# Order of VectorE's last instructions in a graph attention and mixture-of-experts kernel

## The chip, the cores and the metric

One core of one Trainium2 chip runs the whole program. The metric is the device time of one execution in microseconds (us). The engines are TensorE (PE, with its weight loads as PEld), VectorE (DVE), ScalarE (ACT), GpSimd (POOL) and SyncE (SP, which issues most DMAs). Each has its own queue of instructions, and they meet by semaphores.

## The reference

A layer of graph attention on 384 nodes of width 1024 comes first; the change does not touch it. Then comes a mixture of 8 experts, of which each token takes 2:

```python
def _expert(x, g, b, W1, b1, W2, b2, Wo, bo):
    x = _layernorm(x, g, b)
    x1 = x @ W1 + b1
    x2 = jnp.clip(x @ W2 + b2, -20.0, 20.0)
    hidden = jnp.clip(x1 * (x2 * jax.nn.sigmoid(x2)), -10000.0, 10000.0)
    return jnp.clip(hidden @ Wo + bo, -10000.0, 10000.0)
...
scores, idx = jax.lax.top_k(logits, K)
gate = jax.nn.softmax(scores, axis=-1)
...
return (acc + gcol[:, None] * _expert(xf, g, b, w1, bb1, w2, bb2, wo, bbo), None)
...
x = x + _L0_ffn_ref(_layernorm(x, axis=-1)[None], ...)[0]
```

Everything is float32. D is 1024, the hidden width H is 512.

## The kernel before, in words

**Products in two parts.** A float32 operand is split into a high part (`hi`, of a shorter type, copied by ScalarE) and the rest (`lo`, subtracted by VectorE). A product is three matmuls: high by high, high by low, low by high (`three`, line 1206, its matmul on line 1209). The weights come in chunks of 128x2048 (1 MB): SyncE loads a chunk into a raw buffer, ScalarE copies it to `hi` (`split_hi`, line 577, its operation on 581), VectorE subtracts (`split_lo`, line 776, its operation on 778). There are 76 chunks; expert 7's are 68 to 71 (up), and 74 and 75 (down); 72 and 73 are expert 6's down chunks.

**The experts.** Each takes the at most 128 tokens that chose it. For expert `e` TensorE (loop from line 1456) makes the two up projections into banks 1 and 0, then the down projection of expert `e - 1` into banks 3 and 4 (`down`, line 1433: two bias products of line 1439, then per chunk twelve matmuls of line 1209), then turns the hidden activations of expert `e` into bank 2 (line 1451). ScalarE copies bank 2 to the high activations (line 708), VectorE subtracts the low ones (`hidden_lo`, line 1079, operation on 1081). VectorE clips banks 3 and 4 into `y` (`store_y`, line 1084, operation on 1089). `down` waits for the low activations of its expert and for the clip of the expert before (`y_ready`), since both use banks 3 and 4. Then it waits for each of its chunks.

**Adding up.** The outputs of experts 0 to 5 are written to HBM (`ybuf`) by SyncE. Each token gathers its rows back: six gathers of 128 rows (`gather_rows`, line 513, its DMA on 515, issued by GpSimd; three tiles of tokens, two choices each), numbered 0 to 5. VectorE multiplies four of them by the gate and adds them to the residual `xres` (`add_rows`, line 1139, operation on 1143). The gathers 4 and 5 are scaled by ScalarE (line 740) and added to `xres` by GpSimd (line 555).

The outputs of experts 6 and 7 don't go through HBM. They are brought to the tokens by products with one-hot matrices: VectorE builds these (line 1113), TensorE turns them (line 1476) and also makes two columns of gates with twelve one-column products (line 1479); ScalarE copies the turned matrices (line 730), VectorE copies the gate columns (line 1153, `slot_gates`). Expert 6's rows `y` are split with their gate into high rows (ScalarE, line 734) and low rows (VectorE, `y_rest`, line 1146, operation on 1147). Expert 7's rows are clipped in two halves (VectorE, line 1162), then split by halves (ScalarE, line 744; VectorE, `y_rest`). TensorE sums them in six banks (`add_last`, line 1483, matmuls on 1490). VectorE adds the six banks to `xres` (line 1171), and SyncE stores a piece behind each addition (line 423).

**What sets the order.** Each engine's instructions are written out by hand in the order in which it runs them. On VectorE the end is: the clip of the hidden activations of expert 7 (line 1134), splits 74 and 75 (line 1137), low activations of expert 7, clip of expert 6's rows, gate columns, the additions 0, 1 and 2, low rows of expert 6, addition 3, the two clips of expert 7 (which wait for all chunks to be used), the two low halves, and the last six additions. On ScalarE it is: the high activations of expert 7 (708), the turned matrices (730), the high rows of expert 6 (734), the scaling of gathers 4 and 5 (740), the two high halves (744).

Of the kernel before, what the change touches and what calls it, by code (L numbers as in the profile page):

```python
# [41 lines left out]
D = 1024  # L42
# [6 lines left out]
NE = 8  # L49
# [28 lines left out]
CHUNKS = GNN_CHUNKS + len(EXPERT_ORDER)  # L78
# [28 lines left out]
def gnn_ffn(nc, x, src, dst, ety, srcb, dstb, ew, wg, bcols, bo, lng, lnb, lnbc_in, rw, egc, ebc, wf, b1, b2, be, out):  # L107
    ctx = ExitStack()
    with ctx:
        def sem(name):  # L110
            return ctx.enter_context(nc.semaphore(name))
# [147 lines left out]
        slot_gates, y_half, y_hi_done, y_lo_done = sem("slot_gates"), sem("y_half"), sem("y_hi_done"), sem("y_lo_done")  # L259
# [10 lines left out]
        def f0(e):  # L270


            return GNN_CHUNKS + 6 * e - 2

        def up_chunks(e):
            return f0(e) + (2 if e == 0 else 0)
# [51 lines left out]
        def f32(ap):  # L328
            return ap.bitcast(F32)

        def wait_lo(engine, c):

            engine.wait_ge(lo_done, c + 1)
# [434 lines left out]
        def _(dve):  # L768
            chain = [0]

            def link(ins):
                chain[0] += 1
                ins.then_inc(dve_chain, 1)
                dve.wait_ge(dve_chain, chain[0])

            def split_lo(c):
                dve.wait_ge(hi_done, c + 1)
                dve.tensor_tensor(lo[SLOT[c]][:, :], raws[RAW[c]], f32(hi[SLOT[c]][:, :]), ALU.subtract).then_inc(lo_done, 1)  # L778
# [269 lines left out]
            def row_columns():  # L1048

                for j, oh in enumerate((oh1, oh2)):  # L1050
                    link(dve.tensor_tensor(tmp[early], oh[early], pos[early], ALU.mult))
                    link(dve.tensor_reduce(r3[:, 5, :], tmp[early], AX, ALU.add))
                    link(dve.tensor_tensor(tmp[early], oh[early], first_row[early], ALU.mult))
                    link(dve.tensor_reduce(r3[:, 6, :], tmp[early], AX, ALU.add))
                    link(dve.scalar_tensor_tensor(out=r3[:, 3 + j, :], in0=r3[:, 5, :], scalar=float(CAP - 1),
                                                  in1=r3[:, 6, :], op0=ALU.min, op1=ALU.add))
                dve.tensor_copy(rows_u[:, :, :], r3[:, 3:5, :]).then_inc(rows_u_ready, 1)

            def gate_columns():

                dve.wait_ge(gates_ready, 1)
                link(dve.tensor_tensor(over_gate, oh1, wide(r3[:, 8, :]), ALU.mult))
                link(dve.tensor_tensor(tmp, oh2, wide(r3[:, 9, :]), ALU.mult))
                link(dve.tensor_tensor(tmp, tmp, over_gate, ALU.add))
                link(dve.scalar_tensor_tensor(out=over_gate, in0=pos, scalar=float(CAP), in1=tmp, op0=ALU.is_ge, op1=ALU.mult))
                link(dve.scalar_tensor_tensor(out=gates, in0=pos, scalar=float(CAP), in1=tmp, op0=ALU.is_lt, op1=ALU.mult))
                for j, oh in enumerate((oh1, oh2)):
                    link(dve.tensor_tensor(tmp[early], oh[early], gates[early], ALU.mult))
                    link(dve.tensor_reduce(r3[:, 8 + j, :], tmp[early], AX, ALU.add))
                dve.tensor_copy(most[:, :], r3[:, 2, 0:1]).then_inc(most_ready, 1)  # L1070

            def tokens_lo(e, par):
                for a in range(2):
                    half = slice(4 * a, 4 * a + 4)
                    dve.wait_ge(xg_hi_done, 2 * e + a + 1)
                    dve.tensor_tensor(xg_lo[:, par, half, :].rearrange("p k n -> p (k n)"), xg[:, par, a * CW:(a + 1) * CW],
                                      f32(xg_hi[:, par, half, :]).rearrange("p k n -> p (k n)"), ALU.subtract).then_inc(xg_lo_done, 1)

            def hidden_lo(e, par):
                dve.wait_ge(ht_hi_done, e + 1)  # L1080
                dve.tensor_tensor(ht_lo[:, par, :, :].rearrange("p k n -> p (k n)"), B[2],
                                  f32(ht_hi[:, par, :, :]).rearrange("p k n -> p (k n)"), ALU.subtract).then_inc(ht_lo_done, 1)

            def store_y(e, par):

                dve.wait_ge(chunk_used, f0(e + 1) + 6 if e < NE - 1 else CHUNKS)
                if e >= 2:
                    dve.wait_ge(y_stored[par], 16 * (e // 2))
                dve.tensor_scalar(y[:, par, :].rearrange("p (a n) -> p a n", a=2), ps[:, 3:5, :], 10000.0, -10000.0,
                                  ALU.min, ALU.max).then_inc(y_ready, 1)  # L1090
# [9 lines left out]
            for e in range(NE):  # L1100
                nxt = [k if FIRST <= k < CHUNKS else None for k in range(f0(e) + 3, f0(e) + 9)]
                if e:
                    hidden_lo(e - 1, (e - 1) % 2)
                if e >= 2:
                    store_y(e - 2, e % 2)
                if nxt[0]:
                    split_lo(nxt[0])
                if e == NE - 1:

                    wait_lo(dve, UP_LAST)  # L1110
                    for j in range(2):
                        for t in range(NT):
                            ins = dve.tensor_scalar(last_rows[:, j, t, :], slots16[:, :], posm[:, t, LAST[j]:LAST[j] + 1], None, ALU.is_equal)
                    ins.then_inc(last_oh, 1)
                if nxt[1]:
                    split_lo(nxt[1])
                if e == 0:
                    row_columns()
                dve.wait_ge(chunk_used, up_chunks(e) + 2)
                if e:  # L1120
                    dve.wait_ge(h_ready, e)
                dve.tensor_scalar(x2c[:, :], B[1], 20.0, -20.0, ALU.min, ALU.max).then_inc(x2_clipped, 1)
                if e == 0:
                    gate_columns()
                if nxt[2]:
                    split_lo(nxt[2])
                if e + 1 < NE:
                    tokens_lo(e + 1, (e + 1) % 2)
                dve.wait_ge(silu_done, e + 1)
                dve.wait_ge(chunk_used, up_chunks(e) + 4)  # L1130
                if e:
                    dve.wait_ge(h_turned, e)
                link(dve.tensor_tensor(hh[:, :], B[0], sg[:, :], ALU.mult))
                dve.tensor_scalar(hh[:, :], hh[:, :], 10000.0, -10000.0, ALU.min, ALU.max).then_inc(h_ready, 1)
                for k in nxt[3:6]:
                    if k:
                        split_lo(k)

            def add_rows(n):

                t, j = GATHERS[n]
                dve.wait_ge(y_rows_in[j][t], 16)
                link(dve.scalar_tensor_tensor(out=xres[:, t, :], in0=yg[:, YG_SLOT[n], :], scalar=r3[:, 8 + j, t:t + 1],
                                              in1=xres[:, t, :], op0=ALU.mult, op1=ALU.add))

            def y_rest(e, cut):
                dve.scalar_tensor_tensor(out=y_lo[e][:, cut], in0=y[:, e, cut], scalar=slot_gate[:, e:e + 1], in1=f32(y_hi[e][:, cut]),
                                         op0=ALU.mult, op1=ALU.subtract).then_inc(y_lo_done, 1)

            hidden_lo(NE - 1, (NE - 1) % 2)  # L1150
            store_y(NE - 2, (NE - 2) % 2)
            dve.wait_ge(last_oh_turned, 1)
            dve.tensor_copy(slot_gate, B[7][:, 0:2]).then_inc(slot_gates, 1)
            for n in range(3):
                add_rows(n)
            dve.wait_ge(y_hi_done, 1)
            y_rest(0, slice(0, D))
            add_rows(3)
            dve.wait_ge(chunk_used, CHUNKS)
            halves = [slice(0, CW), slice(CW, D)]  # L1160
            for half in range(2):
# [1 line left out]
            for half in range(2):  # L1163
                dve.wait_ge(y_hi_done, 2 + half)
                y_rest(1, halves[half])
            for half in range(2):
                for t in range(NT):
                    dve.wait_ge(last_summed, NT * half + t + 1)
                    if t == NT - 1:
                        dve.wait_ge(tile_added, 1)  # L1170
                    dve.tensor_tensor(xres[:, t, halves[half]], xres[:, t, halves[half]], B[SUM_BANKS[t][half]],
                                      ALU.add).then_inc(out_ready, 1)
# [407 lines left out]
```

## Time and profile before

| what | us |
|---|---|
| three runs | 516.27, 519.77, 518.66 |
| their median | 518.66 |
| the profiled execution's own time | 518.99 |
| its span, from the first to the last instruction | 517.2 |

| engine | busy, share of the span |
|---|---|
| TensorE, matmuls | 93% |
| VectorE | 74% |
| ScalarE | 53% |
| GpSimd | 33% |

The span is what the views of the trace show; the profiled execution's own time is 1.8 us more. A line of a timeline has the start, the duration, the engine, the line of the code, the operation, what is written and read, the shapes and the count; in brackets stands the idle time of the engine before it and what ended that. The duration of merged lines is that from the first start to the last end. Consecutive instructions of VectorE overlap by some hundredths of a microsecond, so a row of 0.68 costs the next one some 0.6 to 0.65. The granted clock of TensorE is 1.00 at 2.4 GHz and 0.50 at 1.2 GHz.

### The profile page before, as it was taken

What the parts mean: (1) busy time and instruction counts of PE and PEld (TensorE: products, weight loads), DVE (VectorE), ACT (ScalarE), POOL (GpSimd) and SP (SyncE); (2) the same over time, 40 slices, a digit from 0 to 9 for tenths busy, and PEclk for the clock granted to TensorE, in tenths of its full rate; (3) what the DMA queues carried; (4) which work ended last, traced back from release to release, by engine and by line L of the source; (5) the groups of instructions that cost most, each with busy time, mean ns of one, the idle gap of its engine ahead of it and who ended that gap; (6) DMA issues with size and microseconds to landing.
All of it is one profiled execution on the core that took longest, in us unless ns stands there. A gap on an engine that the chain in (4) does not pass through costs nothing.

```text
span 517.2 us, 6811 instructions
## 1 busy us (share of the span) xinstructions
PE 482.4 (93%) x2599; PEld 414.2 (80%) x2599; DVE 382.4 (74%) x616; ACT 274.1 (53%) x382; POOL 171.6 (33%) x152
## 2 busy tenths in 40 slices
PE   8999999999999999978899999588999999999984
PEld 8999999999999987755656788467887787877772
DVE  4858989955353342478877987787898898898985
ACT  4725142423433243378785035249769669669531
POOL 5000543764645200456765532420201000000561
PEclk9999999999999999999999998579999999999988
DMA  8489655442424532200055733685788989987553
GB/s 294 161 307 376 167 196 220 164 163 86 148 93 164 169 122 81 81 1 2 1 168 217 284 123 122 207 308 209 303 324 362 398 330 403 352 302 323 182 182 124
DMA packets 21073, 106.33 MB, mean 206 GB/s; under 512 B 4864, under 2 KB 5248, under 8 KB 11312
## 3 DMA queue, kind: packets, MB, share of 16 engines
q1 hardware_dynamic: 15472, 91.53, 47.2%
q0 software_dynamic: 3696, 7.96, 4.8%
q10 hardware_dynamic: 1872, 6.39, 3.7%
q8 instruction: 21, 0.34, 0.3%
q14 instruction: 12, 0.10, 0.1%
HBM read 98.97 MB, written 6.91 MB: 205 GB/s over the span
## 4 chain that ended last, share of the span: by engine, by line
PE 58%; DVE 22%; ACT 10%; DMA 4%; issue 4%; POOL 0%; SPq 0%; DVEq 0%; ACTq 0%; POOLq 0%
PE ps L1209 45%; DVE lo L778 11%; ACT hi L581 4%; ACT xg L695 3%; PE ps L1289 3%; PE ps L1272 3%; PE ps L1300 2%; DMA raw<-in_wg 2%; PE ps L1317 2%; DVE eqt L861 1%; PE ps L1369 1%; DVE pr L878 1%; ACT pr L617 1%; DMA raw<-in_wf 1%; DMA xg<-z_rows,slot_tok 1%
## 5 line engine op out<-in xcount | busy, mean ns | idle before, releaser
L778 DVE TENSOR_TENSOR lo<-raw,hi 128x2048 fp32r<-128x2048 f32 x70 | 161.4, 2328 | 40.4 <-ACT hi L581 40.2
L581 ACT ACTIVATE hi<-raw 128x2048 fp32r<-128x2048 f32 x70 | 131.8, 1913 | 59.0 <-PE ps L1209 46.2
L466 POOL DMA_INDIRECT mask_rows<-colf,bits x48 | 63.1, 1315 | 90.9 <-DVE bits L869 43.6
L497 POOL TENSOR_SCALAR pr<-pr,small 128x384 f32<-128x384 f32 x32 | 40.4, 1275 | 57.8 <-DVE small L884 57.8
L1209 PE MATMUL ps<-xt_hi,lo 128*128 128x384 f32 x176 | 59.1, 336 | 0.0
L1209 PE MATMUL ps<-xt_hi,hi 128*128 128x384 f32 x176 | 59.1, 336 | 0.0
L1209 PE MATMUL ps<-xt_lo,hi 128*128 128x384 f32 x176 | 59.1, 336 | 0.0
L1209 PE MATMUL ps<-hi,xg_hi 128*128 128x512 f32 x128 | 52.0, 406 | 5.7 <-DVE lo L778 3.9
L1209 PE MATMUL ps<-lo,xg_hi 128*128 128x512 f32 x128 | 51.1, 400 | 0.0
L1209 PE MATMUL ps<-hi,xg_lo 128*128 128x512 f32 x128 | 51.1, 399 | 0.0
L1209 PE MATMUL ps<-t_hi,hi 128*128 128x384 f32 x128 | 43.1, 337 | 0.8 <-DVE t_lo L820 0.8
L1209 PE MATMUL ps<-t_hi,lo 128*128 128x384 f32 x128 | 43.0, 336 | 0.0
L1209 PE MATMUL ps<-t_lo,hi 128*128 128x384 f32 x128 | 43.0, 336 | 0.0
L1209 PE MATMUL ps<-hi,t_hi 128*128 128x512 f32 x96 | 39.8, 414 | 0.0
L1209 PE MATMUL ps<-hi,t_lo 128*128 128x512 f32 x96 | 37.9, 395 | 0.0
L1209 PE MATMUL ps<-lo,t_hi 128*128 128x512 f32 x96 | 37.9, 394 | 0.0
L617 ACT ACTIVATE pr<-pr,small 128x384 f32<-128x384 f32 x48 | 29.0, 607 | 14.4 <-DVE small L878 14.4
L1209 PEld LDWEIGHTS ps<-hi,xg_hi 128*128 128x128 f32 x128 | 24.6, 192 | 12.8 <-DVE lo L778 5.4
L525 POOL CAST selx<-sels 128x128 fp32r<-128x128 f32 x8 | 4.4, 551 | 87.3 <-PE ps L1209 86.5
L1209 PEld LDWEIGHTS ps<-xt_hi,lo 128*128 128x128 f32 x176 | 33.1, 188 | 0.0
L1209 PEld LDWEIGHTS ps<-xt_hi,hi 128*128 128x128 f32 x176 | 33.1, 188 | 0.0
L1209 PEld LDWEIGHTS ps<-xt_lo,hi 128*128 128x128 f32 x176 | 33.1, 188 | 0.0
(218 smaller groups left out, 966.8 us busy)
## 6 DMA issues: line engine op xcount, KB each, us to landing
raw<-in_wf SPq DMA_DIRECT2D x42, 1024.0 KB, 7.8
raw<-in_wg SPq DMA_DIRECT2D x28, 1024.0 KB, 4.9
xfb<-in_wf SPq DMA_DIRECT2D x6, 1024.0 KB, 7.2
src_i<-in_srcb ACTq DMA_DIRECT2D x4, 768.0 KB, 3.9
dst_i<-in_dstb ACTq DMA_DIRECT2D x4, 768.0 KB, 7.8
y_rows<-y SPq DMA_DIRECT2D x6, 512.0 KB, 3.0
xin<-in_x SPq DMA_DIRECT2D x3, 512.0 KB, 4.3
xres<-in_x SPq DMA_DIRECT2D x3, 512.0 KB, 4.2
```

The costliest lines, as they stand in the source:

```text
L466: pool.indirect_dma_start(out=mbuf[:, :], out_offset=bass.IndirectOffsetOnAxis(ap=bits[:, 1, g:g + 1], axis=0), in_=colf[:, 5, g:g + 1], i ...
L497: pool.tensor_scalar(pr[:, p % 3, a, i, :], pr[:, p % 3, a, i, :], rinv[:, p % 3, i, a:a + 1], None, ALU.mult).then_inc(normalised, 1)
L581: act.activation(hi[SLOT[c]][:, :], raws[RAW[c]], ACT.Copy).then_inc(hi_done, 1)
L617: act.activation(pr[:, p % 3, a, i, :], pr[:, p % 3, a, i, :], ACT.Exp, scale=-1.0, bias=negmax[:, p % 3, i, a:a + 1], accum_out=rsum[:, p ...
L695: ins = act.activation(xg[:, par, k * P:(k + 1) * P], B[5 + a][:, (k % 4) * P:(k % 4 + 1) * P], ACT.Identity, scale=egb[:, 0, e, k:k + 1], ...
L778: dve.tensor_tensor(lo[SLOT[c]][:, :], raws[RAW[c]], f32(hi[SLOT[c]][:, :]), ALU.subtract).then_inc(lo_done, 1)
L861: ins = dve.scalar_tensor_tensor(out=eqt[:, j % 2, 0:width], in0=keyb[:, j * P:j * P + width], scalar=colf[:, 2, g:g + 1], in1=later[:, 0: ...
L1209: ins = pe.matmul(o, a[s], b[m], start=first and n == 0, stop=last and n == 2)
L1272: ins = pe.matmul(SCORES[n % 2][a][:, 0:N], (q_hi, q_lo)[s][rows, p, tok], (k_hi, k_lo)[m][rows, p, :], start=step == 0, stop=step == 2)
L1289: ins = pe.transpose(TURNED[m % 3][:, i * P:(i + 1) * P], pr[:, p % 3, a, i, j * P:(j + 1) * P], ident[:, :])
L1300: ins = pe.matmul(SUMMED[HD * a:HD * (a + 1), 0:N], val[:, j, cut], at[:, m % 8, :], start=j == 0, stop=j == NT - 1)
L1317: ins = pe.matmul(banks(0)[b][:, 0:N], weight(0, k, slice(b * P, (b + 1) * P))[s], (xt_hi, xt_lo)[m][:, k, :], start=n == 0 and k == 0, st ...
```

## The change

Only VectorE's program changes. In the loop of the experts, the last weight split (chunk 75) is left out. Behind the loop the clip of expert 6's rows now comes first, then the low activations of expert 7, the gate columns, split 75, the low rows of expert 6, the additions 0, 1 and 2. The fourth addition (`add_rows(3)`) moves from behind the low rows of expert 6 to behind the two low halves of expert 7.

```diff
                 for k in nxt[3:6]:
-                    if k:
+                    if k and k < CHUNKS - 1:
                         split_lo(k)
...
+            store_y(NE - 2, (NE - 2) % 2)
             hidden_lo(NE - 1, (NE - 1) % 2)
-            store_y(NE - 2, (NE - 2) % 2)
             dve.wait_ge(last_oh_turned, 1)
             dve.tensor_copy(slot_gate, B[7][:, 0:2]).then_inc(slot_gates, 1)
+            split_lo(CHUNKS - 1)
+            dve.wait_ge(y_hi_done, 1)
+            y_rest(0, slice(0, D))
             for n in range(3):
                 add_rows(n)
-            dve.wait_ge(y_hi_done, 1)
-            y_rest(0, slice(0, D))
-            add_rows(3)
             dve.wait_ge(chunk_used, CHUNKS)
             halves = [slice(0, CW), slice(CW, D)]
             for half in range(2):
...
             for half in range(2):
                 dve.wait_ge(y_hi_done, 2 + half)
                 y_rest(1, halves[half])
+            add_rows(3)
             for half in range(2):
                 for t in range(NT):
                     dve.wait_ge(last_summed, NT * half + t + 1)
```

## Rows read from the trace of the kernel before

**Rows 1.** The page, busy time of each engine

```profile
PE 482.4 (93%) x2599; PEld 414.2 (80%) x2599; DVE 382.4 (74%) x616; ACT 274.1 (53%) x382; POOL 171.6 (33%) x152
```

**Rows 2.** Chain of waits that ended last (start, us, what), from 440 us

```profile
466.87 2.80 PE ps L1209 x12
...
494.55 1.22 DVE y L1089
...
496.61 7.16 PE ps L1209 x24
...
505.35 2.13 DVE lo L1147
```

**Rows 3.** Timeline of VectorE, from 470 us

```profile
489.55 4.48 DVE L778 TENSOR_TENSOR lo<-raw,hi 128x2048 fp32r<-128x2048 f32 x2
493.95 0.68 DVE L1081 TENSOR_TENSOR ht_lo<-ps,ht_hi 128x512 fp32r<-128x512 f32 x1
494.55 1.21 DVE L1089 TENSOR_SCALAR y<-ps 128x1024 f32<-128x1024 f32 x1
...
495.75 3.91 DVE L1143 SCALAR_TENSOR_TENSOR xres<-yg,r,xres 128x1024 f32<-128x1024 f32 x3
...
500.90 1.28 DVE L1143 SCALAR_TENSOR_TENSOR xres<-yg,r,xres 128x1024 f32<-128x1024 f32 x1
503.87 1.29 DVE L1162 TENSOR_SCALAR y<-ps 128x512 f32<-128x512 f32 x2 [1.68 <-PE ps L1209]
...
508.30 3.67 DVE L1171 TENSOR_TENSOR xres<-xres,ps 128x512 f32<-128x512 f32 x6 [0.17 <-PE ps L1490]
```

**Rows 4.** Timeline of TensorE, from 470 us

```profile
491.28 0.40 PE L1209 MATMUL ps<-hi,ht_lo 128*128 128x512 f32 x1
...
492.61 1.40 PE L1479 MATMUL ps<-r,xfb 128*128 128x1 f32 x12
495.91 0.70 PE L1439 MATMUL ps<-brow,selx 128*128 128x512 f32 x2 [1.91 <-DVE y L1089]
```

**Rows 5.** One stretch: us, busy (count) by engine, granted clock (PEclk), DMA, GB/s

```profile
498.00:499.00 1.00, 1.00 (x4) 0.80 (x3) 0.96 (x2) 0.00 (x0) 0.00 (x0) 0.50 1.06 360
```

**Rows 6.** Timeline of ScalarE, from 470 us

```profile
492.15 0.60 ACT L708 ACTIVATE ht_hi<-ps 128x512 fp32r<-128x512 f32 x1 [1.50 <-PE ps L1451]
494.04 0.87 ACT L730 ACTIVATE hi<-ps 128x384 fp32r<-128x384 f32 x2 [1.29 <-PE ps L1479]
...
500.47 1.16 ACT L740 ACTIVATE yg<-yg,r 128x1024 f32<-128x1024 f32 x1 [3.44 <-DMA yg<-y_rows,rows_u]
501.94 1.15 ACT L740 ACTIVATE yg<-yg,r 128x1024 f32<-128x1024 f32 x1 [0.31 <-DMA yg<-y_rows,rows_u]
504.59 1.34 ACT L744 ACTIVATE hi<-y,r 128x512 fp32r<-128x512 f32 x2 [1.50 <-DVE y L1162]
```

**Rows 7.** Timeline of GpSimd: the last three gathers' issue, and its two additions

```profile
492.95 1.90 POOL L515 DMA_INDIRECT yg<-y_rows,rows_u  x1 [0.30 <-issue]
495.15 0.94 POOL L515 DMA_INDIRECT yg<-y_rows,rows_u  x1 [0.30 <-issue]
496.40 1.44 POOL L515 DMA_INDIRECT yg<-y_rows,rows_u  x1 [0.30 <-issue]
501.71 2.74 POOL L555 TENSOR_TENSOR xres<-xres,yg 128x1024 f32<-128x1024 f32 x1 [3.87 <-ACT yg L740]
504.54 2.38 POOL L555 TENSOR_TENSOR xres<-xres,yg 128x1024 f32<-128x1024 f32 x1
```

**Rows 8.** View of line 515, the six gathers: from issue to landing

```profile
DMA to landing us min/median/max: 5.2/6.0/6.3
```

**Rows 9.** Timelines of GpSimd and VectorE from 283 us, outside the change

```profile
283.35 2.39 POOL L490 TENSOR_TENSOR xres<-xres,x2sg 128x1024 f32<-128x1024 f32 x1 [2.68 <-DVE lo L778]
...
285.69 4.47 POOL L490 TENSOR_TENSOR xres<-xres,x2sg 128x1024 f32<-128x1024 f32 x1
...
283.50 4.40 DVE L778 TENSOR_TENSOR lo<-raw,hi 128x2048 fp32r<-128x2048 f32 x1 [0.23 <-ACT hi L581]
```

## The prediction

> **What bounds the kernel now.** I read the page first: TensorE is busy for 93% of the span [rows 1], so elsewhere in the program time on VectorE matters only where TensorE waits for it. The change touches only the last 28 us, so I read the chain of waits there. The reader is to see that it changes engines: it runs over VectorE's clip of expert 6's rows (494.55), TensorE's last 24 weight products, then VectorE's first low half (505.35) [rows 2]. The timeline of each engine then shows why.
>
> VectorE is without a gap from 489.55 to 502.18, has one gap of 1.68 us before 503.87 (it waits for TensorE), and ends its last addition at 508.30 + 3.67 = 511.97 [rows 3]. TensorE stands idle for 1.91 us before 495.91, since its last down projection needs expert 6's rows clipped out of banks 3 and 4, and the clip stands behind two splits on VectorE [rows 3, 4]. After that gap the granted clock is 0.50 in 498 to 499, 1.2 of 2.4 GHz [rows 5]. So 24 products with their two bias products take 503.8 - 495.9 = 7.9 us, where twelve at the full clock took 2.80 us earlier [rows 2]: 24 would be 5.6.
>
> ScalarE and GpSimd are the third part. Behind TensorE's end VectorE clips two halves, but ScalarE's high halves can only follow when it has scaled the two gathered tiles whose rows landed at 500.47 and 501.94 [rows 6]. GpSimd adds these tiles to the residual, from 501.71 and from 504.54 [rows 7].
>
> **The change, step by step.** Nothing is added or removed: the same instructions stand in another order on one engine. No DMA is issued by the moved code; SP's queue waits for nothing that moves except the last six additions; GpSimd's queue holds no moved instruction, but I come to it.
>
> 1. *Clip and low half ahead of split 75.* VectorE ends split 74 at 489.55 + 2.28 = 491.8. TensorE's last product of expert 6 ends at 491.28 + 0.40 = 491.7 [rows 4], so the clip starts at 491.8 at once and is done at 493.0 (1.21 [rows 3]). The high half of the activations is there at 492.15 + 0.60 = 492.75 [rows 6]; the low half takes 0.65 and ends at 493.65 [rows 3]. Now a wait stands ahead of split 75: the copy of the two gate columns needs TensorE's twelve column products, which end at 492.61 + 1.40 = 494.0 [rows 4]. So VectorE idles 0.4 us, and behind that wait stands split 75, 494.1 to 496.4.
>
> 2. *TensorE.* Both things it waited for are there at 493.65, so it starts when its own queue is through, at 494.05 in place of 495.91: 1.85 us sooner. It needs chunk 75 after its two bias products (0.7) and twelve others (2.8), at 497.55; the split ends at 496.4. That is 1.15 us of cover; a split later than that would cost what it is late. I take the full clock, since the gap that came before the half clock is gone: end at 494.05 + 0.7 + 5.6 = 500.35, 3.4 us sooner. At the half clock for as long as before it is 1.6 more, 501.95. Both ends are covered, as step 4 shows.
>
> 3. *VectorE up to the clips.* ScalarE's first high rows come at 494.04 + 0.87 + 1.16 = 496.1 (two copies, then a tile of 1.16 as at 500.47 [rows 6]). So the low rows of expert 6 (1.28, as an addition of their size [rows 3]) follow the split without a wait, 496.35 to 497.6, and three additions of 1.28 bring VectorE to 501.5 (3.91 for three [rows 3]). This is later than TensorE's 500.35: the gap of 1.68 is gone and VectorE is what is late next. The two clips run 501.5 to 502.8, 2.35 us sooner than before.
>
> 4. *What is late after that: ScalarE, through the gathers.* The gathers' own issue on GpSimd takes 0.94 when VectorE reads PSUM (495.15, under the clip). It is held while VectorE runs a split: the one from 492.95 ended at 494.85, 0.8 after the split that ended at 494.03; the one from 496.40 ended 0.8 after an addition had ended at 497.03 [rows 3, 7]. In the new order the fourth gather lies under the clip and the low half and ends at 493.9; the fifth starts at 494.2, just behind the start of split 75 at 494.1, and is held until 496.4 + 0.8 = 497.2; the sixth lies under the low rows, 497.5 to 498.4. From issue to landing the six took 5.2 to 6.3 us [rows 8]. For the fifth, held as long as any, I take 6.3: 500.5, as before. The sixth lands near 502. ScalarE scales the fifth by 501.7 and the sixth by 503.2, and only then makes the high halves, to 504.6. So TensorE's 3.4 us and VectorE's 2.35 us arrive at ScalarE as little more than 1.4 (504.59 before [rows 6]).
>
> 5. *The two additions of GpSimd and the low halves.* In the trace before, the first low half took 2.13 us at 128x512, where 1.28 buys twice the size on an addition: it stood from 505.35 until GpSimd's second addition had ended at 504.54 + 2.38 = 506.92, then took 0.6 [rows 2, 7]. The same pair of kinds meets earlier in the trace: at 283.50 a split waited 2.1 us for GpSimd's addition from 283.35, and then GpSimd's next, from 285.69, waited 2.1 us for that split [rows 9]. So one holds off the other, and whoever waits comes in between two instructions of the other engine. Put in order: GpSimd's first addition 501.8 to 504.2; first low half (asked for at 503.95) 504.2 to 504.85; GpSimd's second 504.85 to 507.25; second low half to 507.9. If GpSimd's second comes ahead of both halves, the sum is the same, since the four simply queue. Before, it was 508.13: a gain of 0.2 is left. The price per half lies between 0 and 2.38; I take the queue, because both rows above show it for these kinds.
>
> 6. *The fourth addition moved behind the halves.* Before it lay ahead of VectorE's gap of 1.68 and cost nothing. Its new place is on the path: 507.9 + 1.28 = 509.2. TensorE's last sums would be ready by then (first half from 504.9 on), so nothing covers it. The last six additions follow, 3.67: 512.85, against 511.97.
>
> Sum: -0.2 (halves), -0.15 (the wait of the last additions), +1.28 (fourth addition) = **+0.9 us**. The rest of the span after the last addition (517.2 - 511.97, the last stores) stays. The profiled execution's own time was 518.99, so it would be 519.9; that one lies 0.33 above the median of the three runs, 518.66, and by the median I say **519.6 us**.
>
> At step 4 the trace and a rule differ. [Rows 7] show the gathers' issue held by splits and additions that VectorE makes of two SBUF operands. The Trainium skill ("SBUF — State Buffer", section "Who interferes with whom") says of VectorE's `tensor_tensor` that it "takes only the pair's read interface, and descriptor generation needs the write interface: inferred"; by it the fifth gather would not be held. What that gives is worked out from rows as the second rival below. The measurement decides here, and it says held; the chance of the rival comes from how close 494.1 and 494.2 are.
>
> **The rivals.** *The low halves don't queue with GpSimd* (faster). Then the halves end at 505.2, the fourth addition at 506.5, the last at 510.15: -1.8 us, 516.8. For it: the clips, read from PSUM, took 0.65 each (1.29 for both) under GpSimd's first addition, undisturbed [rows 3, 7], and the halves need only come in other moments. Against it: both rows of step 5.
>
> *The fifth gather gets in ahead of split 75.* Then it takes 0.94 and lands 5.2 us after 494.2, at 499.4; ScalarE is done with it at 500.55, but VectorE's third addition runs to 501.5 and holds GpSimd's off until then. First addition 501.5 to 503.9, first half 504.55, second addition 506.9, second half 507.55, fourth addition 508.85, last 512.5: +0.5, 519.2. For it: 0.1 us decides. Against it: GpSimd would have to be early.
>
> *The last gathers land later* (slower). Everything in step 5 hangs on the start of GpSimd's first addition, one us for one us, from 501.8 on. The fifth gather now leaves GpSimd 1.1 us later than before (497.2 against 496.1), and before it landed 4.4 us after leaving. By that it lands at 501.6, the first addition starts at 502.85 and the last ends at 513.9: +1.9, 520.6. For it: 4.1 and 4.4 are the times from leaving to landing of the last two [rows 6, 7]. Against it: those two stood behind other gathers' rows, and the fifth no longer does.
>
> *The change doesn't do what it says:* TensorE's gap stays, because the column products and not the clip end last, or split 75 is late by more than 1.15 us. Then TensorE ends as before, the clips come at 503.8, the halves as before at 508.1, and the fourth addition still costs 1.28: +1.1, 519.8. The products' end at 494.0 speaks against it.
>
> **How the numbers follow.** Forecast (+0.9) 0.50; halves not queued (-1.8) 0.18; fifth gather first (+0.5) 0.14; gathers late (+1.9) 0.15; gap stays (+1.1) 0.03. The cases span 516.8 to 520.6. The three runs lie between 2.4 below and 1.1 above their median, and I add a part of this at either end: 516.0 to 521.5; the forecast's own range is 518.6 to 520.6. About 1%, 5.2 us, is what a measurement of this kernel can tell from no change. No case reaches it: even all 3.4 us of TensorE would not. Outside lie surprises alone, 0.02 faster and 0.03 slower.
>
> **What would show it.** Right: TensorE's bias products of line 1439 start near 494.05 with no idle time before them; the granted clock stays at 1.00 to 501; no idle time on VectorE before line 1162, which starts near 501.5; a low half of line 1147 of some 2.4 to 3 us beside GpSimd's line 555; the fourth addition ending near 509.2. Wrong: both low halves at 0.65 and the last addition before 511; the fifth gather issued in 0.94; an idle gap inside TensorE's 24 products; a time outside 516 to 521.5.

## The result, and the profile after

The changed kernel took 520.75 us by the median of 22 runs, against 518.86 of 22 runs of the kernel before: a ratio of 1.0031 (1.0021 to 1.0042), 1.1 to 2.2 us more. That is no change by the bound of 1%, and slower by what so many runs can tell. Two later comparisons of the same pair, with 12 runs of the changed kernel each, gave 1.0017 (0.9998 to 1.0036) and 1.0012 (0.9996 to 1.0028). The forecast was 519.6, +0.9 us; the profiled execution after has a span of 518.3 against 517.2.

The changed kernel has one line more ahead of VectorE's last additions and of TensorE's code, so TensorE's 1209, 1439 and 1490 are now 1210, 1440 and 1491, and VectorE's 1171 is 1172. This is the timeline of VectorE after (start, duration, then as before), which answers to [rows 3]:

```profile
489.60 2.28 DVE L778 TENSOR_TENSOR lo<-raw,hi 128x2048 fp32r<-128x2048 f32 x1
491.80 1.22 DVE L1089 TENSOR_SCALAR y<-ps 128x1024 f32<-128x1024 f32 x1
492.93 0.68 DVE L1081 TENSOR_TENSOR ht_lo<-ps,ht_hi 128x512 fp32r<-128x512 f32 x1
494.05 0.16 DVE L1153 COPY r<-ps 128x2 f32<-128x2 f32 x1 [0.44 <-PE ps L1480]
494.12 2.28 DVE L778 TENSOR_TENSOR lo<-raw,hi 128x2048 fp32r<-128x2048 f32 x1
496.32 1.28 DVE L1147 SCALAR_TENSOR_TENSOR lo<-y,r,hi 128x1024 fp32r<-128x1024 f32 x1
497.52 3.92 DVE L1143 SCALAR_TENSOR_TENSOR xres<-yg,r,xres 128x1024 f32<-128x1024 f32 x3
501.48 1.29 DVE L1162 TENSOR_SCALAR y<-ps 128x512 f32<-128x512 f32 x2
504.48 3.51 DVE L1147 SCALAR_TENSOR_TENSOR lo<-y,r,hi 128x512 fp32r<-128x512 f32 x2 [1.71 <-ACT hi L744]
507.91 1.27 DVE L1143 SCALAR_TENSOR_TENSOR xres<-yg,r,xres 128x1024 f32<-128x1024 f32 x1
509.22 3.68 DVE L1172 TENSOR_TENSOR xres<-xres,ps 128x512 f32<-128x512 f32 x6
```

The wait of 1.68 us for TensorE ahead of the clips is gone, and a wait of 1.71 us for ScalarE has come behind them. The clips start 2.4 us sooner; the two low halves, which took 2.78 us under GpSimd's second addition, now take 3.51 and end at 507.99 in place of 508.13. The fourth addition follows them, so the last addition ends at 512.90, not 511.97.

TensorE after, which answers to [rows 4]: no idle time ahead of the bias products, and a new gap ahead of expert 7's sums.

```profile
492.61 1.40 PE L1480 MATMUL ps<-r,xfb 128*128 128x1 f32 x12
493.87 0.71 PE L1440 MATMUL ps<-brow,selx 128*128 128x512 f32 x2
...
499.77 0.39 PE L1210 MATMUL ps<-hi,ht_lo 128*128 128x512 f32 x1
...
507.38 0.79 PE L1491 MATMUL ps<-hi 128*128 128x512 f32 x1 [4.50 <-DVE lo L1147]
```

The down projection ends at 500.16, 3.6 us sooner. That lead ends in a gap of 4.50 us. Two stretches after, with the granted clock third from the right (as [rows 5]):

```profile
497.00:498.00 1.00, 1.00 (x6) 0.82 (x5) 1.00 (x2) 0.00 (x0) 0.70 (x2) 1.00 0.39 98
508.00:509.00 1.00, 1.00 (x4) 0.81 (x3) 1.00 (x1) 0.00 (x0) 0.00 (x0) 0.50 0.00 0
```

In this profile the half clock has not gone but moved: from the 24 products to the sums behind the new gap. Two more profiles of the changed kernel (below) differ here: the sums of the second half run at 0.50 again in one, and in the other the granted clock stays at 1.00, where TensorE waited 2.35 and then 1.13 us. The last two gathers, GpSimd's additions and ScalarE's scaling, which answer to [rows 6, 7]:

```profile
494.24 2.98 POOL L515 DMA_INDIRECT yg<-y_rows,rows_u  x1 [0.30 <-issue]
497.52 0.94 POOL L515 DMA_INDIRECT yg<-y_rows,rows_u  x1 [0.30 <-issue]
502.00 2.36 POOL L555 TENSOR_TENSOR xres<-xres,yg 128x1024 f32<-128x1024 f32 x1 [3.54 <-ACT yg L740]
504.44 2.33 POOL L555 TENSOR_TENSOR xres<-xres,yg 128x1024 f32<-128x1024 f32 x1
```
```profile
500.75 1.16 ACT L740 ACTIVATE yg<-yg,r 128x1024 f32<-128x1024 f32 x1 [4.79 <-DMA yg<-y_rows,rows_u]
502.68 1.15 ACT L740 ACTIVATE yg<-yg,r 128x1024 f32<-128x1024 f32 x1 [0.77 <-DMA yg<-y_rows,rows_u]
```

The fifth gather's issue is held under split 75 (2.98 us, ending 0.82 after the split ended at 496.40). GpSimd's second addition, 504.44 to 506.77, came 0.04 us ahead of the first low half, which stood until it was through.

### The profile page after: what moved, and what is told of

It is laid out like the page before. It is cut to its first block, busy times and chain, and to the rows that moved or that the text cites. A ratio compares the mean times of both kernels' runs of the same rounds, so it can differ in the third digit from the quotient of the medians.

```text
span 518.3 us, 6811 instructions
## 1 busy us (share of the span) xinstructions
PE 481.6 (93%) x2599; PEld 413.6 (80%) x2599; DVE 383.1 (74%) x616; ACT 273.9 (53%) x382; POOL 169.3 (33%) x152
## 4 chain that ended last, share of the span: by engine, by line
PE 55%; DVE 21%; ACT 10%; DMA 6%; issue 4%; POOL 3%; ACTq 0%; SPq 0%; DVEq 0%; POOLq 0%
PE ps L1210 42%; DVE lo L778 10%; ACT hi L581 4%; ACT xg L695 3%; PE ps L1290 3%; PE ps L1273 3%; PE ps L1301 2%; POOL yg L515 2%; DMA raw<-in_wg 2%; PE ps L1318 2%; DVE eqt L861 1%; PE ps L1370 1%; DVE pr L878 1%; DMA yg<-y_rows,rows_u 1%; ACT pr L617 1%
## 5 line engine op out<-in xcount | busy, mean ns | idle before, releaser
L466 POOL DMA_INDIRECT mask_rows<-colf,bits x48 | 61.9, 1290 | 92.5 <-DVE bits L869 44.3
```

The source lines that it names most:

```text
L466: pool.indirect_dma_start(out=mbuf[:, :], out_offset=bass.IndirectOffsetOnAxis(ap=bits[:, 1, g:g + 1], axis=0), in_=colf[:, 5, g:g + 1], i ...
```

## The experiments

Executions reach the tail at times up to 2 us apart, so the profiles are compared from a mark that all share: the start of split 74 (489.55 before). To the end of the last addition it is 22.42 us before and 23.30 after; such figures of each run, worked out from its timelines, stand in the table at the end of this section.

**One part alone: the fourth addition moved, the rest as before.**

```diff
             y_rest(0, slice(0, D))
-            add_rows(3)
             dve.wait_ge(chunk_used, CHUNKS)
...
                 y_rest(1, halves[half])
+            add_rows(3)
```

> The kernel before, with its fourth addition alone moved behind the two low halves. Theory (one queue): the low halves of VectorE and the two additions of GpSimd pass one after the other, so the halves end near 507.9 with or without the addition ahead of them, and its 1.28 us come on top: last addition ends near 512.75, 0.8 us later than before (ratio 1.0015). Rival (the early split is what costs): no difference, within 0.3 us of before, since TensorE, ScalarE and the splits stand as they did. Rival (clock): over 1.3 us later, if TensorE's last sums run at the half clock and end after VectorE.

Ratio 1.0013 (0.9995 to 1.0030); last addition 22.85 us from the mark, 0.43 later than before. The halves end 0.63 sooner from the mark (17.95 against 18.58), and the addition itself costs its 1.27. The sign is as the queue says, the size half; the time alone can't tell it from nothing. The 0.63 has two sources, which this run doesn't part. GpSimd's first addition is no longer held by the fourth of VectorE (2.42 us, not 2.74). And TensorE, after the same wait for the clip as before, keeps the full clock this time (third from the right again), so the clips come 1.64 sooner from the mark and the first low half gets in between GpSimd's two additions:

```profile
497.28 0.70 PE L1439 MATMUL ps<-brow,selx 128*128 128x512 f32 x2 [1.95 <-DVE y L1089]
498.00:499.00 1.00, 1.00 (x6) 0.78 (x6) 0.96 (x2) 0.39 (x1) 1.00 (x1) 1.00 0.93 369
```
```profile
503.60 1.29 DVE L1161 TENSOR_SCALAR y<-ps 128x512 f32<-128x512 f32 x2 [1.25 <-PE ps L1209]
505.09 3.78 DVE L1147 SCALAR_TENSOR_TENSOR lo<-y,r,hi 128x512 fp32r<-128x512 f32 x2 [0.20 <-ACT hi L744]
```

So the half clock of the one profile of before does not follow each such gap, and some 1.6 of the 3.6 us that TensorE gains there came here without the early clip.

**The other part alone: the changed kernel with the fourth addition ahead of the clips.**

```diff
                 add_rows(n)
+            add_rows(3)
             dve.wait_ge(chunk_used, CHUNKS)
...
                 y_rest(1, halves[half])
-            add_rows(3)
```

> The changed kernel with its fourth addition put back ahead of the two clips; the early clip, low activations and late split stay. Theory (one queue): the addition now lies at 501.5 to 502.8 and holds GpSimd's first addition until then; the halves end near 508.8 and the last addition near 512.4: 0.45 us sooner than the changed kernel, 0.45 later than before (ratio 1.0009). Rival (the fourth addition was all the loss): 1.3 us sooner than the changed kernel, level with before or 0.2 better.

Ratio 1.0012 (0.9995 to 1.0030). The last addition ends 22.35 us from the mark: 0.95 sooner than in the changed kernel, level with before. Timeline of its VectorE:

```profile
503.84 1.29 DVE L1163 TENSOR_SCALAR y<-ps 128x512 f32<-128x512 f32 x2
505.50 3.92 DVE L1147 SCALAR_TENSOR_TENSOR lo<-y,r,hi 128x512 fp32r<-128x512 f32 x2 [0.38 <-ACT hi L744]
509.35 3.66 DVE L1172 TENSOR_TENSOR xres<-xres,ps 128x512 f32<-128x512 f32 x6
```

Here the rival was nearer than my theory (0.45): by the profile the moved addition is all of the loss, and the early clip and late split, which gave TensorE 3.6 us, are worth nothing at the end (22.35 against 22.42), with the halves again at 3.92 us in GpSimd's queue. The times alone can't show it: 1.0012 lies inside the intervals of the two later comparisons of the changed kernel.

**GpSimd's additions cut short.**

```diff
-ins = pool.tensor_tensor(xres[:, t, :], xres[:, t, :], yg[:, YG_SLOT[n], :], ALU.add)
+ins = pool.tensor_tensor(xres[:, t, 0:8], xres[:, t, 0:8], yg[:, YG_SLOT[n], 0:8], ALU.add)
```

> The changed kernel with GpSimd's two additions cut to 8 of 1024 columns: most of the sum for one choice of the third tile of tokens is left out. Theory (one queue): nothing holds the low halves, each takes some 0.65; ScalarE gives the first high half at 504.5, so the halves end at 505.8, the fourth addition at 507.1 and the last addition at 510.8: 2.1 us sooner than the changed kernel, 1.2 sooner than before (ratio 0.998). Rival (ScalarE and the landing of the gathers set the end): within 0.3 us of the changed kernel. Rival (clock): some 1 us sooner, since TensorE's last twelve sums at the half clock then end at 510.3 to 510.8 and not VectorE's work.

Ratio 0.9987 (0.9962 to 1.0012). Its VectorE:

```profile
505.88 1.41 DVE L1147 SCALAR_TENSOR_TENSOR lo<-y,r,hi 128x512 fp32r<-128x512 f32 x2 [1.76 <-ACT hi L744]
```

Both halves together now take 1.41 us, not 3.51, and the last addition ends 21.24 from the mark, 2.06 sooner than in the changed kernel: what was expected to 0.1. ScalarE still ends the wait ahead of them, so its part of step 4 stands beside that queue.

**The fourth addition in VectorE's gap.**

```diff
+            add_rows(3)
             for half in range(2):
                 dve.wait_ge(y_hi_done, 2 + half)
                 y_rest(1, halves[half])
-            add_rows(3)
```

> The changed kernel with its fourth addition between the two clips and the low halves, where its VectorE stands idle for 1.7 us. Theory (one queue): the gap is no gap for an addition of two SBUF operands, since GpSimd's first addition runs through it; the fourth addition waits for that, the low halves and GpSimd's second addition queue behind, and the last addition ends within 0.4 us of the changed kernel. Rival (the gap is free): 1.2 us sooner than the changed kernel, 0.3 sooner than before.

Ratio 1.0043 (1.0023 to 1.0063); last addition 24.98 us from the mark, 1.7 later than in the changed kernel. Neither expectation. VectorE:

```profile
502.04 2.88 DVE L1143 SCALAR_TENSOR_TENSOR xres<-yg,r,xres 128x1024 f32<-128x1024 f32 x1
504.95 3.37 DVE L1147 SCALAR_TENSOR_TENSOR lo<-y,r,hi 128x512 fp32r<-128x512 f32 x2
508.97 0.69 DVE L1172 TENSOR_TENSOR xres<-xres,ps 128x512 f32<-128x512 f32 x1 [0.65 <-PE ps L1491]
509.82 0.69 DVE L1172 TENSOR_TENSOR xres<-xres,ps 128x512 f32<-128x512 f32 x1 [0.17 <-PE ps L1491]
...
513.24 0.69 DVE L1172 TENSOR_TENSOR xres<-xres,ps 128x512 f32<-128x512 f32 x1 [0.16 <-PE ps L1491]
```
```profile
508.00:509.00 1.00, 1.00 (x3) 0.81 (x3) 0.35 (x2) 0.00 (x0) 0.00 (x0) 0.50 0.00 0
```

The queue is there: the addition takes 2.88 us in place of 1.28, and the gap was no gap. But TensorE then stands idle for 5.47 us, its sums run at 0.50, and each last addition waits for TensorE and comes 0.86 us after the one before, not 0.6. My theory had left the clock out; here it decides. In the first profile of the changed kernel the sums at the half clock just keep up, because the fourth addition lies ahead of the last six.

**The fifth gather let in ahead of split 75.**

```diff
             dve.wait_ge(last_oh_turned, 1)
+            for _ in range(3):
+                link(dve.tensor_copy(slot_gate, B[7][:, 0:2]))
             dve.tensor_copy(slot_gate, B[7][:, 0:2]).then_inc(slot_gates, 1)
```

> The changed kernel with the copy of the two gate columns made four times over, each waiting for the one ahead, so that split 75 starts some 0.5 us later, behind the start of the fifth gather's issue. Theory (the splits hold the gathers' issue): the fifth gather is issued in 0.94 us and not 2.98, and its rows land 5.2 us after the start of its issue, some 1 us sooner than in the changed kernel; its gain is held back by VectorE's third addition, and the last addition ends within 0.5 us of the changed kernel. Rival (the issue of a gather takes long for another reason, as its own place in the order): 2.5 us or more again.

There is one profile of this version and no comparison of times; last addition 22.92 us from the mark, 0.38 sooner than in the changed kernel, with the added copies in it. Its last two gathers:

```profile
495.05 0.93 POOL L515 DMA_INDIRECT yg<-y_rows,rows_u  x1 [0.30 <-issue]
496.29 2.36 POOL L515 DMA_INDIRECT yg<-y_rows,rows_u  x1 [0.30 <-issue]
```

The fifth takes 0.93, not 2.98, and now the sixth is held under the split (495.56 to 497.84) and leaves 0.81 after it. So a split does hold a gather's issue. The Trainium skill's inference in "SBUF — State Buffer" ("Who interferes with whom"), that a `tensor_tensor` leaves descriptor generation alone, is not borne out by these rows for a gather. Among what the rows of a gather read stands `rows_u`, its row numbers in SBUF; whether that read or the making of descriptors is held they don't show. The rows of the fifth landed only some 0.45 us sooner, 6.1 us after the start of the issue and not 5.2.

**The changed kernel again, plain, twice.**

> The changed kernel once more, beside the others of this call. By its profile, from the start of split 74 to the end of the last addition, it loses 0.9 us to the kernel before (ratio 1.0017); by the first measurement 1.6 (1.0031). Theory (one queue): in a profile the first low half waits for GpSimd's second addition or stands between the two, and the last addition ends some 23.3 us after the start of split 74. Rival (clock): the profile shows TensorE's last twelve sums ending later than VectorE's fourth addition allows, and the last addition with a wait ahead of it.

> The changed kernel a third time, as the measure for the next one. Theory (queue and clock): 0.9 us over before in executions in which TensorE's last sums keep up (ratio 1.0017), up to 2 in those in which they run at the half clock behind a late first half; 1.002 to 1.003 on the whole. A look at its last additions shows which it is: back to back every 0.6 us, or one per 0.86 with a wait on TensorE.

The ratios are given above; last addition 23.69 and 23.28 us from the mark. In both the first low half stands between GpSimd's two additions and the last additions follow each other every 0.6 us. So in three profiles the tail is 0.9 to 1.3 us longer than in the one of before, and in none does TensorE's clock hold up an addition.

**The changed kernel with 16 idle products in TensorE's gap, twice.**

```diff
             add_last(0, (0, 1), True)
+            pe.wait_ge(y_half, 1)
+            keep_busy(16, B[3])
```

> The changed kernel with 16 idle products (0.24 us each) on TensorE between the sums of expert 6 and those of expert 7, so that it doesn't stand idle for 4.5 us. Theory (one queue): VectorE's fourth addition and GpSimd's port set the end; the granted clock stays at 1.00, the last sums are done sooner, and the time stays within 0.3 us of the changed kernel in the same call. Rival (clock): the half clock is the rest of the measured loss; 0.6 us or more sooner than the changed kernel.

> The changed kernel with the 16 idle products again, beside the plain one. Theory (queue and clock): the granted clock stays at 1.00 and every last addition follows the one before; 0.5 to 1.5 us sooner than the plain one in this call. Rival (queue alone): within 0.3 us of it, and the first comparison was chance.

Ratios 0.9987 (0.9971 to 1.0002) and 0.9985 (0.9966 to 1.0003), by the medians 1.3 and 2.3 us below the plain one timed beside them (518.51 against 519.85; 518.20 against 520.49), by the ratios 1.6 and 1.4, though the intervals still meet. The granted clock stays at 1.00 to the end of the sums. That is about the size expected if the half clock made up the loss, but the clock is not its reason: the last addition ends 23.26 and 23.08 us from the mark, hardly sooner than 23.28 to 23.69. What differs more is the time behind the last addition: 2.9 and 3.0 us to the end of the span, where the three plain profiles have 5.4, 3.0 and 5.2. That this makes up the difference of the times is likely but not shown, since one plain profile has the short end too. The view of line 342, the branch over the block for crowded experts that TensorE takes at its end, shows where the profiles differ: first of the plain kernel (third time), then of the second one with idle products.

```profile
L342 PEldq COMPARE_BRANCH  x1: 3698/3698/3698, 514.8 to 514.8; - x1
```
```profile
L342 PEldq COMPARE_BRANCH  x1: 458/458/458, 513.9 to 513.9; - x1
```

**A version made from these: fourth addition ahead of the clips, GpSimd's second addition behind the low halves, the third tile's pieces last.** Twice plain, once with 9 idle products ahead of expert 7's sums.

```diff
# GpSimd, for gather 5
+                        if n == 5:
+                            pool.wait_ge(y_lo_done, 3)
...
# VectorE: add_rows(3) ahead of the clips, as above; VectorE's additions and SyncE's stores
-            for half in range(2):
-                for t in range(NT):
+            for half, t in LAST_PIECES:
...
+        LAST_PIECES = [(0, 0), (0, 1), (1, 0), (1, 1), (0, 2), (1, 2)]
```

> The order of the run before last (fourth addition ahead of the clips), and GpSimd's second addition waits until both low halves are done, with the third tile's two pieces last among the six additions and stores. Theory (one queue): GpSimd's second addition lies under additions that read PSUM, which it doesn't hold; halves end at 506.4, four additions at 508.8, GpSimd's second at 508.75, the last at 510.1: 1.9 us sooner than before (ratio 0.9964). Rival (clock): TensorE stands idle for 2.9 us before its last twelve sums; at the half clock they take 5.1 us from 505.8, so the last addition ends at 511.5, 0.5 sooner than before. Rival (ScalarE and the gathers set the end): level with the changed kernel.

> The version with the fourth addition ahead of the clips and GpSimd's second addition behind the low halves, a second time. Theory (one queue): 1.2 to 1.9 us sooner than before (ratio 0.9964 to 0.9977). Rival (chance in the first comparison): level with before.

> The same version with 9 idle products of 0.24 us on TensorE ahead of the sums of expert 7. Theory (queue and clock): its gap of 2.7 us is shorter and its first half comes early, so the clock costs it little: 0 to 0.6 us sooner than without them. Rival (clock alone): 1 us or more sooner.

Ratios 0.9977 (0.9959 to 0.9994), 0.9965 (0.9949 to 0.9980), and with idle products 0.9949 (0.9933 to 0.9964). The last addition ends 20.66, 20.67 and 20.65 us from the mark: 1.75 sooner than before (1.9 expected) and 2.6 sooner than the changed kernel. From the first profile, VectorE, then GpSimd (its code stands three lines further down: 1150 is 1147, 1174 the last additions, 558 is 555):

```profile
505.00 1.81 DVE L1150 SCALAR_TENSOR_TENSOR lo<-y,r,hi 128x512 fp32r<-128x512 f32 x2 [0.32 <-ACT hi L747]
506.96 3.87 DVE L1174 TENSOR_TENSOR xres<-xres,ps 128x512 f32<-128x512 f32 x6 [0.16 <-PE ps L1493]
```
```profile
503.23 2.36 POOL L558 TENSOR_TENSOR xres<-xres,yg 128x1024 f32<-128x1024 f32 x1 [4.18 <-ACT yg L743]
506.98 2.39 POOL L558 TENSOR_TENSOR xres<-xres,yg 128x1024 f32<-128x1024 f32 x1 [1.39 <-DVE lo L1150]
```

TensorE waits 2.72 us ahead of the last sums, but the granted clock stays at 1.00, so the clock rival did not come. GpSimd's second addition runs in full under the additions that read PSUM and costs them next to nothing (3.87 against 3.67). The idle products bring nothing to the last addition (20.65 against 20.67), and their version too has the short branch (0.45 us), so its further gain lies behind the last addition. By the times this version is 0.2 to 0.5% faster than before, clear of noise though inside the bound of 1%, and the changed kernel is none the faster in any comparison.

| kernel | clips start | low halves end | last addition ends | from there to the end of the span |
|---|---|---|---|---|
| before | 14.32 | 18.58 | 22.42 | 5.2 |
| changed (three profiles) | 11.88 | 18.4 to 18.8 | 23.3 to 23.7 | 5.4, 3.0, 5.2 |
| fourth addition alone | 12.68 | 17.95 | 22.85 | 5.3 |
| order alone | 13.18 | 18.76 | 22.35 | 5.3 |
| short GpSimd additions | 11.87 | 16.34 | 21.24 | 2.9 |
| in the gap | 11.88 | 19.37 | 24.98 | 5.1 |
| gather first | 12.48 | 18.01 | 22.92 | 5.4 |
| 16 idle products (two) | 11.9 | 18.3, 18.2 | 23.3, 23.1 | 2.9, 3.0 |
| new version (plain, plain, idle products) | 13.2 | 16.6 | 20.7 | 5.3, 5.1, 4.1 |

Times are us from the start of split 74, but for the last column.

## Why the prediction was right

Steps 1 to 3 came out within 0.2 us: clip at 491.80, split 75 at 494.12 behind a wait of 0.44, bias products at 493.87 (494.05 forecast), the end of the down projection at 500.16 at the full clock (500.35), the clips at 501.48 (501.5). Step 4: the fifth gather was held and left at 497.22 (497.2); ScalarE had its rows at 500.75 (500.5) and those of the sixth at 502.68 (502), so the high halves ended at 505.06, later than the 504.6 of the sum, and it cost nothing, since the queue of step 5 was longer. Step 5: the halves ended at 507.99 (507.9); GpSimd's second addition came ahead of both, an order that the step had named as having the same sum. Step 6: the fourth addition cost its 1.27, and the last ended at 512.90 (512.85). The run with short GpSimd additions shows step 5 by itself (2.06 us), and that with the order alone shows step 6 (0.95 of its 1.28). One premise of step 6 was not quite so: the fourth addition's old place was not free, since there it held GpSimd's first addition (2.74 us, against 2.42 with it alone moved).

The first rival, halves that don't queue, falls with the run of short additions. The second, the fifth gather first, was not what happened, but when it was forced it gave 0.38 us against the 0.4 worked out. That the size fits is partly luck: the rows landed 0.45 us sooner and not the 1.1 that the rival took, and the added copies made VectorE's third addition end 0.6 later. The third, gathers that land late, happened in part: in the second profile ScalarE had the fifth's rows 11.87 us from the mark and not 11.15, and the last addition ended 0.39 later, not one us for one us as step 5 had it. The fourth, that TensorE's gap stays, did not happen.

What fell short is the size. The first comparison says 1.1 to 2.2 us, and 0.9 lies just under it; the two later ones agree with 0.9 but hold zero too. Two terms were missing. The sum took the clock as settled once the first gap was gone, and did not ask about the gap that TensorE's lead opens further on; in the three profiles of the changed kernel that cost nothing, and in the run with the addition in the gap the last addition came 1.7 us later. And it took the time behind the last addition as fixed, where it is some 5.2 or 2.9 us. Whether either makes up the rest in the many executions without a profile is open.

## What to carry to other kernels

An instruction that frees an engine sooner is worth what the last wait of the stage leaves of it: here 3.6 us on TensorE ended in a wait for gathered rows and in the queue between VectorE's two-operand work on SBUF and GpSimd's additions. Before moving work out of a gap, look at what the other engine runs there and at what will lie behind the new place; work that reads PSUM is where a GpSimd addition can hide (3.87 us for six additions over one, 3.67 without). A lead given to TensorE that opens a gap later can come back as the half clock, as it did behind gaps of 4.50 and 5.47 us; behind 1.9 us it came in one profile and not in another.

## What the runs showed of the hardware that was not expected

TensorE's last branch took 3.68 to 3.86 us in nine profiles and 0.35 to 0.46 in five, and with it the span ended 5.1 to 5.4 or, but for one, 2.9 to 3.0 us after the last addition. The same changed kernel showed both (3.86 and 3.70, and 0.46), so it is not set by the program alone; all three profiles with idle products, which add instructions to TensorE's program, had the short one, and only two of the eleven profiles without them. What sets it was not tried. The one exception is the new version with idle products: its branch was short, yet the span ended 4.1 us after the last addition, since GpSimd's closing drain, 7.68 us from 507.4 on, ended last:

```profile
L109 POOLq DRAIN  x1: 7678/7678/7678, 507.4 to 507.4; - x1
```

That row starts with GpSimd's second addition (507.48 to 509.88) and is 5.47 us where that addition was cut short. So in this version it is likely GpSimd's late addition that the end of the program waits for next.
